# The last four routing tiles taken together, and three steps of exponentials in flight in self-attention

## The reference, cut to what matters

```python
# L0: route 1601 context rows into 2048 states, then a gated update
tok = ctx @ W_proj + b_proj
attn = softmax(x @ tok.T / 16)
routed = attn @ tok
ps_n, in_n = ln(x), ln(routed)
u, r = sigmoid([ps_n, in_n] @ W_u + b_u), sigmoid([ps_n, in_n] @ W_r + b_r)
cand = tanh([r * ps_n, in_n] @ W_n + b_n)
x = ln((1 - u) * x + u * cand)
# L1: a transformer block, 16 heads of 16
x = x + mha(ln1(x), ln1(x)); x = x + mha(ln2(x), ctx)
x = x + gelu(ln3(x) @ w1.T + b1) @ w2.T + b2
```

## Time and profile before

| what | value |
|---|---|
| median of 3 runs | 1500.87 us (1500.01 to 1504.94) |
| profiled execution, its own time | 1502.36 us |
| its span in the trace | 1500.7 us |
| mean granted TensorE clock | 0.967 |
| PE busy | 1397.3 us (93%) |
| ACT busy | 1095.9 us (73%) |
| DVE busy | 596.3 us (40%) |

### The profile page before, as it was taken

The page is one execution under the profiler, slowest core; times in us unless marked ns, Lnnn a source line. Parts: engine busy times, 40 slices in busy tenths (PEclk is TensorE's granted clock), DMA queues, the critical chain, the costliest instruction groups (busy, mean ns, idle before and its releaser), DMA issues.

```text
span 1500.7 us, 20741 instructions
## 1 busy us (share of the span) xinstructions
PE 1397.3 (93%) x8014; PEld 635.9 (42%) x8014; DVE 596.3 (40%) x1394; ACT 1095.9 (73%) x1350; POOL 48.7 (3%) x63
## 2 busy tenths in 40 slices
PE   7999989998669999999999999899898999899887
PEld 5667776776422223222322322222233433433346
DVE  5556576676740204312332340343342243144133
ACT  2533435444339999999999999789788797788843
POOL 2000000000010000000000000000000000000000
PEclk9999999998879999999999999899999999999999
DMA  9400001001249200100010353511000000000000
GB/s 305 164 34 1 1 0 57 1 1 57 89 117 126 67 16 19 26 28 11 12 53 12 45 118 47 119 36 35 13 23 15 23 12 12 23 15 1 5 11 15
DMA packets 35048, 66.06 MB, mean 44 GB/s; under 512 B 6202, under 2 KB 20092, under 8 KB 34204
## 3 DMA queue, kind: packets, MB, share of 16 engines
q1 hardware_dynamic: 29580, 43.24, 13.5%
q0 software_dynamic: 5360, 21.37, 3.9%
HBM read 42.70 MB, written 22.02 MB: 43 GB/s over the span
## 4 chain that ended last, share of the span: by engine, by line
PE 68%; ACT 22%; DVE 6%; issue 4%; DMA 1%; DVEq 0%; POOL 0%; SPq 0%; ACTq 0%; POOLq 0%
PE PS L1339 20%; ACT PX L897 20%; PE PS L1322 14%; PE PS L1421 3%; PE PS L1389 2%; PE PS L1139 2%; PE PS L1127 2%; PE PS L1370 2%; PE PS L1130 2%; PE PS L1056 2%; PE PS L1095 2%; PE PS L1096 1%; PE PS L1097 1%; PE PS L960 1%; PE PS L1404 1%
## 5 line engine op out<-in xcount | busy, mean ns | idle before, releaser
L897 ACT ACTIVATE PX<-PS 128x1024 f32<-128x1024 f32 (+1 forms) x928 | 881.7, 1040 | 119.6 <-PE PS L1322 73.3
L1339 PE MATMUL PS<-PX,V 128*32 128x512 f32 (+1 forms) x3712 | 499.3, 610 | 5.0 <-ACT PX L897 3.0
L1322 PE MATMUL PS<-QST,stack 50*128 50x512 f32 (+1 forms) x1856 | 385.5, 472 | 21.8 <-issue 13.5
L1322 PEld LDWEIGHTS PS<-QST,stack 50*128 50x128 f32 (+1 forms) x1856 | 156.8, 185 | 394.6 <-ACT PX L897 327.5
L1918 DVE COPY OT<-PS 128x512 f32<-128x512 f32 x32 | 22.1, 692 | 299.6 <-PE PS L1339 296.0
L1339 PEld LDWEIGHTS PS<-PX,V 128*32 128x32 f32 (+1 forms) x3712 | 73.7, 108 | 150.0 <-issue 111.6
L766 ACT ACTIVATE PH<-PS 128x512 fp32r<-128x512 f32 (+1 forms) x52 | 31.2, 600 | 82.7 <-PE PS L1076 73.2
L1421 PE MATMUL PS<-W,HIDT 128*128 128x256 f32 x192 | 47.8, 392 | 9.7 <-ACT HIDT L883 9.7
L1953 DVE RECIPROCAL REC<-REC 128x256 f32<-128x256 f32 x30 | 52.6, 1753 | 1.0
L782 ACT ACTIVATE TR<-PS,small 128x128 f32<-128x128 f32 x32 | 10.0, 363 | 56.7 <-PE PS L1130 56.7
L1421 PEld LDWEIGHTS PS<-W,HIDT 128*128 128x128 f32 x192 | 34.5, 189 | 33.7 <-issue 30.0
(11 more groups left out here) (209 smaller groups left out, 1574.2 us busy)
## 6 DMA issues: line engine op xcount, KB each, us to landing
QST<-q_parts SPq DMA_DIRECT2D x192, 64.0 KB
q_parts<-PARTS POOLq DMA_DIRECT2D x16, 512.0 KB, 3.5
stack<-k_parts SPq DMA_DIRECT2D x24, 200.1 KB, 6.8
stack<-k_parts SPq DMA_DIRECT2D x18, 256.0 KB
k_parts<-KPARTS POOLq DMA_DIRECT2D x8, 512.0 KB, 3.2
v_cross<-V POOLq DMA_DIRECT2D x1, 3328.0 KB, 11.8
V<-v_cross SPq DMA_DIRECT2D x2, 1664.0 KB, 13.6
k_parts<-PARTS POOLq DMA_DIRECT2D x6, 512.0 KB, 3.3
```

The source lines that it names most:

```text
L897: act.activation(PX[0:kr, (2 * t + half) % 4, :, :], PS[0:kr, slot:slot + 2, :], ACT.Exp, scale=SCALE).then_inc(at["exp"], 1)
L1322: ins = pe.matmul(PS[0:kr, 2 * (n % LOOK) + jj, :], KST[a][lo:lo + NROW, pair, kt * P:kt * P + kr].bitcast(F32R), QST[lo:lo + NROW, pair, ...
L1339: ins = pe.matmul(PS[32 * j:32 * j + 32, 6, :], V[0:kr, kt, 2 * (g // 2 * GH + j) + g % 2, :], PX[0:kr, (2 * t + j // 2) % 4, j % 2, :], s ...
```

## The change

1. **The last four tiles** (12 to 15) leave the slots: slots end at 15, and `last_tiles` on PE, ACT and DVE replaces slots 16 to 22. They are routed into four banks (6, 4, 5, 3) at once. DVE takes mean and variance from PSUM without dividing first, and one `rsqrt` over six values serves all four; ACT writes the normalised blocks (`routed_hat`) in place of DVE. Gates, candidates and finishes alternate between tiles, with CF4, XHS4, TR4, RPS4, TU4, CD4 and E4 (in the space of CHI, CLO and CN) as separate buffers. The projections of chunks 1 to 3 are placed anew.
2. **stage3** puts the k norm ahead of both q units, the banks rotate otherwise, and ACT's `split` no longer waits for `parts_ready`. For the first chunk `self_shift` drops a copy, and POOL stores its shift before the q parts of the last chunk. POOL's memset of V becomes eight smaller ones.
3. **Self-attention** gets six half-buffers (PX and PX2, which lies where KPARTS and W1 were), so ACT waits for pv(t-3). W1 is loaded after self-attention's last pv.
4. **PE's order in self-attention** becomes `scores(2t+2); pv(t-1); scores(2t+3); pieces`. The score slots rotate across chunk ends.
5. **REST[0]** spreads the pieces more widely.

```diff
-    {"y": [5, 8, 11, 14], "h": [21, 23], "u": [26, 28, 30, 32], "n": [38, 40]},
+    {"y": [6, 9, 12, 15], "h": [21, 24], "u": [27, 31, 38, 42], "n": [52, 56]},
...
-HAT_STEP = (16, 13)
+HAT_STEP = (17, 13)
...
+    PX2 = m.put("PX2", [P, 2, 2, CHUNK], F32, oW1)
...
+    def route_bank(i):
+        return 6 if i < FIRST_LAST else (6, 4, 5, 3)[i - FIRST_LAST]
+    def gate_bank(i):
+        return 7 if i < FIRST_LAST else (6, 4, 5, 7)[i - FIRST_LAST]
...
+    def score_slot(a, h):
+        return 2 * ((a * HALVES + h) % LOOK)
+    def exp_place(a, h):
+        if a == 1:
+            return PX[:, (h + 2) % 4]
+        return PX2[:, h % 6 - 4] if h % 6 >= 4 else PX[:, h % 6]
...
-                       enumerate(ks + vs[:2] + qs[:1] + norms[:1] + qs[1:] + vs[2:] + norms[1:])])
+        stage3.append([... enumerate(ks + vs[:2] + norms[:1] + qs + vs[2:] + norms[1:])])
...
-                sp.wait_ge(S["ln1_T"], TILES)
+            else:
+                sp.wait_ge(A[0]["pv"], HALVES // 2)
...
+                gp.wait_ge(S["l0_scaled"], 1)
+                for n in range(TILES // 2, TILES):
+                    gp.memset(v_parts(n, P)[:, :, 1:3, :], 1.0).then_inc(S["v_cleared"], 1)
...
+                if half and i == CHUNKS - 1:
+                    store_shift(0, 0, 0)
...
-            wait(act, S["parts_ready"], u - 1)
...
+        def routed_hat(i):
+            j = i - FIRST_LAST
+            act.wait_ge(S["l0_scaled"], 1)
+            act.activation(XHS4[:, j, 1, :], PS[:, route_bank(i), 0:D], ACT.Identity, scale=sm(SC4 + j),
+                           bias=sm(SB4 + j)).then_inc(S["l0_hat"], 1)
...
-                            wait(act, at["pv"], c * steps + t - 1)
+                            wait(act, at["pv"], c * steps + t + 1 - PLACES[a] // 2)
...
+        def last_tiles():                      # on PE
+            a, b, c, e = LASTS
+            for i in range(LAG):
+                l0_pv(STEPS - LAG + i)
+            gates(a - 1)
+            for i in LASTS:
+                route(i)
+            candidate(a - 1)
+            qkv(FIRST[0:2]); h_transposed(a - 3); qkv(FIRST[2:5])
+            hats(a); hats(b); gates(a); hats(c); gates(b); candidate(a); h_transposed(a - 2)
+            hats(e); gates(c); h_transposed(a - 1); candidate(b); gates(e); qkv(FIRST[5:6])
+            candidate(c); qkv(FIRST[6:8]); candidate(e); qkv(FIRST[8:]); qkv(SECOND[0:8])
+            for i in LASTS:
+                h_transposed(i)
+            qkv(SECOND[8:]); qkv(THIRD)
...
-                wait(pe, at["exp"], h - 1 if n < 2 else h - 2)
+                wait(pe, at["exp"], h - 2)
...
+                    if a == 0 and 2 * t + 3 < 2 * steps:
+                        scores(c, 2 * t + 3, first)
                     for o, kind, i, part, last in ev[t]:
...
-                    if 2 * t + 3 < 2 * steps:
+                    if a == 1 and 2 * t + 3 < 2 * steps:
                         scores(c, 2 * t + 3, first)
...
+        def last_tiles():                      # on DVE
+            norms(None, a - 2, a - 3); finish(a - 2, into=four[5]); gates(a - 1)
+            for i in LASTS:
+                routed_stats(i)
+            routed_scales(); next_hat(a - 2, AG4 + 10, NY4 + 5); candidate_sum(a - 1); new_state(a - 1, four[4])
+            rsqrt4(1, 4); finish(a - 1, AG4 + 8, NY4 + 4, four[6]); gates(a); qkv(FIRST[0:4]); gates(b)
+            candidate_sum(a); qkv(FIRST[4:5]); new_state(a, four[0]); rsqrt4(1, 6); next_hat(a - 1, ...); gates(c)
+            candidate_sum(b); new_state(b, four[1]); gates(e); candidate_sum(c); qkv(FIRST[5:6])
+            new_state(c, four[2]); candidate_sum(e); qkv(FIRST[6:8]); new_state(e, four[3]); rsqrt4(TPC)
+            finish(a, ...); qkv(FIRST[8:]); finish(b, ...); qkv(SECOND[0:2]); finish(c, ...); finish(e, ...)
+            rsqrt4(TPC); next_hat(a, ...); next_hat(b, ...); qkv(SECOND[2:5]); next_hat(c, ...); next_hat(e, ...)
+            qkv(SECOND[5:]); qkv(THIRD[0:2] + THIRD[4:5] + THIRD[2:4] + THIRD[5:])
```

More of the change, by code:

```diff
@@ L779, in reset @@
             act.wait_ge(S["l0_gates"], i + 1)
[L780 removed]
+            tr = work_of(i)[0]
+            if i < FIRST_LAST:
+                wait(act, S["l0_rps"], i)
             for c in range(2):
[L782 removed]
+                ins = act.activation(tr[:, c, :], PS[:, gate_bank(i), c * P:(c + 1) * P], ACT.Tanh, bias=sm(BRH + c),
+                                     scale=0.5)
             ins.then_inc(S["l0_rtanh"], 1)
@@ L809, in candidate @@
             act.wait_ge(S["l0_candz"], i + 1)
-            act.activation(CD[:], CZ[:], ACT.Tanh).then_inc(S["l0_cand"], 1)
+            _, _, _, _, cz, cd, _ = work_of(i)
+            act.activation(cd, cz, ACT.Tanh).then_inc(S["l0_cand"], 1)
+        def last_tiles():
+            a, b, c, e = LASTS
+            routed_out(CHUNKS - 1)
+            reset(a - 1)
+            update(a - 1)
+            for i in LASTS:
+                state_hat(i)
+            qkv(FIRST[0:2])
+            h_taken(a - 3)
+            for i in (e, a, b, c):
+                routed_hat(i)
+            candidate(a - 1)
+            concat(a)
+            concat(b)
+            reset(a)
+            update(a)
+            concat(c)
+            reset(b)
+            update(b)
+            candidate(a)
+            h_taken(a - 2)
+            concat(e)
+            reset(c)
+            update(c)
+            h_taken(a - 1)
+            candidate(b)
+            reset(e)
+            update(e)
+            qkv(FIRST[5:6])
+            candidate(c)
+            qkv(FIRST[6:7])
+            candidate(e)
+            qkv(SECOND)
+            for i in LASTS:
+                h_taken(i)
+            qkv(THIRD)
         def slot(k):
@@ L869, in slot @@
                 h_taken(h)
-        for k in range(SLOTS):
+        for k in range(TILES):
             slot(k)
@@ L1789, in candidate, with routed_stats, rsqrt4, routed_scales @@
-            stats(E2[:], 0, ch)
+            candidate_sum(g)
+            new_state(g)
+        def routed_stats(i):
+            j = i - FIRST_LAST
+            ve.wait_ge(S["l0_routed"], i + 1)
+            ch(ve.reciprocal(sm(RS4 + j), PS[:, route_bank(i), D:D + 1]))
+            stats(PS[:, route_bank(i), 0:D], j, ch, STAT4, AG4)
+        def rsqrt4(n, first=0):
+            rsqrt(n, ch, ag=AG4 + 2 * first, y=sm(NY4 + first, n), tmp=TMP4)
+        def routed_scales():
+            pairs = sm(AG4, 2 * TPC).rearrange("p (n two) -> p n two", two=2)
+            mean, var = (pairs[:, :, i:i + 1].rearrange("p n o -> p (n o)") for i in range(2))
+            for _ in range(2):
+                ch(ve.tensor_tensor(var, var, sm(RS4, TPC), ALU.mult))
+            rsqrt4(TPC + 2)
+            ch(ve.tensor_tensor(sm(SC4, TPC), sm(NY4, TPC), sm(RS4, TPC), ALU.mult))
+            ve.scalar_tensor_tensor(out=sm(SB4, TPC), in0=mean, scalar=-1.0, in1=sm(SC4, TPC), op0=ALU.mult,
+                                    op1=ALU.mult).then_inc(S["l0_scaled"], 1)
+            ve.wait_ge(S["l0_scaled"], 1)
@@ new lines, in last_tiles @@
+        def last_tiles():
+            a, b, c, e = LASTS
+            four = [(j, STAT4, AG4) for j in range(7)]
+            norms(None, a - 2, a - 3)
+            finish(a - 2, into=four[5])
+            gates(a - 1)
+            for i in LASTS:
+                routed_stats(i)
+            routed_scales()
+            next_hat(a - 2, AG4 + 10, NY4 + 5)
+            candidate_sum(a - 1)
+            new_state(a - 1, four[4])
+            rsqrt4(1, 4)
+            finish(a - 1, AG4 + 8, NY4 + 4, four[6])
+            gates(a)
+            qkv(FIRST[0:4])
+            gates(b)
+            candidate_sum(a)
+            qkv(FIRST[4:5])
+            new_state(a, four[0])
+            rsqrt4(1, 6)
+            next_hat(a - 1, AG4 + 12, NY4 + 6)
+            gates(c)
+            candidate_sum(b)
+            new_state(b, four[1])
+            gates(e)
+            candidate_sum(c)
+            qkv(FIRST[5:6])
+            new_state(c, four[2])
+            candidate_sum(e)
+            qkv(FIRST[6:8])
+            new_state(e, four[3])
+            rsqrt4(TPC)
+            finish(a, AG4, NY4, four[0])
+            qkv(FIRST[8:])
+            finish(b, AG4 + 2, NY4 + 1, four[1])
+            qkv(SECOND[0:2])
+            finish(c, AG4 + 4, NY4 + 2, four[2])
+            finish(e, AG4 + 6, NY4 + 3, four[3])
+            rsqrt4(TPC)
+            next_hat(a, AG4, NY4)
+            next_hat(b, AG4 + 2, NY4 + 1)
+            qkv(SECOND[2:5])
+            next_hat(c, AG4 + 4, NY4 + 2)
+            next_hat(e, AG4 + 6, NY4 + 3)
+            qkv(SECOND[5:])
+            qkv(THIRD[0:2] + THIRD[4:5] + THIRD[2:4] + THIRD[5:])
@@ L1795, in slot @@
             n = LT * b + (3 * j + 1 if j else 0)
-            if b >= CHUNKS:
-                norms(r, f, h)
-                gates(g)
-                finish(f)
-                qkv(LATE.get(k - 1, ()))
-                qkv(EARLY.get(k, ()))
-                candidate(g)
```

(1 more changed line is left out.)

233 lines of the change are left out of this document (137 added, 96 removed).

## The result

The changed kernel takes 1489.67 us (median of 5 runs, 1487.89 to 1492.73), the kernel before 1500.87. The ratio is 0.9931, with a 95% interval of 0.9913 to 0.9949. It is faster, by 11 us and not by the 27 of the forecast, and lies just above the forecast's range (1462 to 1488). The profiled execution took 1488.8 us, with a span of 1487.1.

What follows compares the result with a forecast made beforehand. Bounds: a chain hopping between engines in the tail, and self-attention near ACT's floor, losing time to PE's pieces. Gains 13.4 (tail) + 13.5 + 0.4 (self-attention) = 27.3 us off 1502.4; less 1.5 to the median, 1474 us, range 1462 to 1488.

Steps and rivals of the forecast that it cites:

- The tail: Last context product to first scores: 18.4 us shorter at full clock, less 5 for the clock, gains 13.4 us (6 to 18).
- (d): Tail: four times transpose and copy through bank 2, 5.4 us, ending at 401.3 us.
- (e): Tail: PE's last v, norms and THIRD take 13.6 us, with DVE behind it 15.6, ending at 416.9 us.
- the clock's share: Tail: 5 us (0 to 12) taken off for half clock, expected in part of (e) and something of an earlier stretch.
- (c): Tail: DVE's last new state, two rsqrt, four finishes and work between them, 19.6 us, ending at 395.9 us.
- R2: Rival: the tail stays as long and only self-attention gains, 1487 us; chance 0.08.
- R4: Slower rival: PE at 1.2 GHz from the tail's second stretch through (e), 10 us slower, 1511 us; chance 0.03.
- The gap from the flag to the first scores: End of the tail: 6.1 us for flag, register load and first matmul, claimed to stay.
- the ledger of self-attention: Tally of PE's lateness: pieces add cost, each step removes 0.18 us, ACT loses the excess; gain taken as 4.5 us a chunk.
- allowance of 1.25 us: Self-attention: PE lateness the three score slots tolerate after the change; new REST then loses 2.7 us a chunk.
- allowance of 0.27 us: Self-attention before: PE lateness tolerated with two buffer steps, fitted so the old REST loses 7.85 us against measured 7.5.
- R1: Rival: score slots, not PX, hold ACT; self-attention stays at 126 us, only the tail counts, 1487.5 us; chance 0.10.

Runs made afterwards that it cites:

- e10: Changed kernel with the first chunk's shift stored after the last q parts, as before: 1487.77 us, ratio 0.9892.
- e5: Changed kernel with the old order of scores and pieces, and the second u part at step 30 instead of 31: 1478.80 us, ratio 0.9841.
- e3: Changed kernel with the old order of scores and the old REST, keeping the third step of buffer: 1481.63 us, ratio 0.9862.
- e4: Changed kernel with only REST and HAT_STEP put back, keeping three steps of buffer and the new order: 1486.91 us, ratio 0.9915.
- e2: Changed kernel with only the old order of scores and pieces put back, keeping three steps and the new REST: 1481.35 us, ratio 0.9874.
- e7: Changed kernel with only the second u part moved, to step 30 instead of 31: 1485.27 us, ratio 0.9885.
- e6: e7 with both scores of a step issued side by side ahead of pv, pieces behind them: 1478.43 us, ratio 0.9841.
- e1: Changed kernel with self-attention's part put back (four places, old order, old REST), leaving the tail alone: 1490.63 us, ratio 0.9939.
- e11: Kernel before with e5's self-attention alone and W1's load moved, tail as before: 1490.06 us, ratio 0.9920.
- e9: e5 with three y pieces and both n pieces moved (y at 6, 10, 14, 16; n at 53, 55): 1479.52 us, ratio 0.9835.
- e8: Changed kernel with half of pv between the two scores of every step, so no two scores stand together: 1749.98 us, ratio 1.164.

## Why the prediction was wrong, step by step

**The tail was right in its sum, in part by luck.** The forecast had 13.4 us. From the last context product's start (326.06 before, 322.80 after) to the first scores (441.37, 424.72) it is 115.3 and 101.9 us, 13.4 less. Three timeline rows of the changed kernel, which answer to the earlier trace rows: the last copy of h, the last norm's reduction, the first scores.

```profile
401.22 0.81 ACT L804 ACTIVATE hF<-PS,cols 128x128 f32<-128x128 f32 x2 [0.90 <-PE PS L1133]
...
417.82 0.68 DVE L1834 TENSOR_REDUCE small<-PS 16x1 f32<-16x512 f32 x1
...
424.72 1.65 PE L1444 MATMUL PS<-QST,stack 50*128 50x512 f32 x6 [5.44 <-issue]
```

Windows from (d) of the prediction, the last four transposes, on: (d), then (e).

```profile
395.30:402.03 6.73, 3.58 (x11) 2.29 (x12) 4.37 (x9) 3.23 (x8) 1.45 (x2) 0.50 0.58 169
402.03:418.50 16.47, 13.59 (x40) 6.99 (x39) 9.96 (x19) 7.16 (x12) 3.43 (x5) 0.91 0.46 163
```

The tail itself began 3.26 us earlier than in the profile before, and the forecast counted from 326.3. On the forecast's scale the last copy ends at 402.0 + 3.3 = 405.3, where (d) had 401.3 before the clock's share. The last reduction ends at 418.5 + 3.3 = 421.8, where (e) had 416.9 and 5 for the clock, 421.9. So the 5 us that were set aside for the clock came out in sum, but not where they were put. The first of the four transposes starts at 395.30 + 3.3 = 398.6, where (c) ended at 395.9, so 2.7 us are there before (d), in a stretch with a granted clock of 0.91 to 0.97. That it is the clock's doing there is not shown. In (d) the clock is 0.50, and it takes 6.7 us in place of 5.4. In (e), where the forecast had most of the half clock, it is 0.91, and only 0.9 us are added. The granted clock of the tail was 0.88, up from 0.84. The last four transposes do stand together (L1133 at 395.30, 397.04, 398.75 and 400.46), each with its copy at 1.71 us, where the sum had 1.36. R2 (the tail stays as long) and R4 (half clock throughout) fall.

**The gap from the flag to the first scores stayed**, at 424.72 - 419.32 = 5.40 us from the decision's reduction (before, 441.37 - 436.10 = 5.27; the two reductions below, changed kernel and before), and the shift's load is not what ends it (e10).

```profile
419.32 0.16 DVE L2082 TENSOR_REDUCE small<-PS 1x1 f32<-1x16 f32 x1 [0.39 <-PE PS L1363]
...
436.10 0.16 DVE L1874 TENSOR_REDUCE small<-PS 1x1 f32<-1x16 f32 x1 [0.39 <-PE PS L1242]
```

**The step that failed is the ledger of self-attention**: with an allowance of 1.25 us the new `REST` was to lose 2.7 us a chunk, which, with a margin for pv, was taken as a gain of 4.5 us in each of three chunks. Measured is a gain of 0. Three terms of it were wrong:

- The allowance of 1.25 us. The prediction held that the wait for pv was the tight one and that the three score slots left room. It read one wait behind a y, 0.29 us for pv. But the kernel before has two there. Between the rows that the earlier trace rows show stands this one:

```profile
588.59 1.03 ACT L897 ACTIVATE PX<-PS 128x1024 f32<-128x1024 f32 x1 [0.34 <-PE PS L1322]
```

ACT waits 0.34 us for scores (L1322), and one exponential later 0.29 us for pv, and so behind all four y of the chunk. The allowance of 0.27 us was fitted to both losses together and put down to pv alone. The third step of buffer takes away only the second of them. What stays is the wait for scores, as e5 shows at the first y of a chunk:

```profile
556.85 3.80 ACT L992 ACTIVATE PX<-PS 128x1024 f32<-128x1024 f32 x4
560.99 2.86 ACT L992 ACTIVATE PX<-PS 128x1024 f32<-128x1024 f32 x3 [0.33 <-PE PS L1444]
```

The four exponentials start 0.91 us apart, and the next one comes 4.14 us after the first of them in place of 3.64. ACT so loses 0.50 us to a y of 1.06, and by the ledger's rule the allowance of the score slots is 0.56 us and not 1.25. The reason for the difference is that 1.25 was worked out for the first scores of two that stand side by side. The second can't be issued before one more exponential has ended, and behind it in PE's queue stand the pv of 1.00 us and the piece, before the scores that ACT needs next. The text saw that pv lowers the allowance and took only 0.6 us a chunk off for it. With 0.55 us the same ledger loses some 5.5 us a chunk with the old `REST` and 4.5 with the new (estimates, from the prediction's own costs). Measured, over the 118.6 us of its floor, are 5.1 (e3) and 4.1 (e5). The third step of buffer gains 2.4 us a chunk (e3), where the prediction's ledger gave 7.85 - 4.2 = 3.7 with the old `REST`.
- The order of the scores, which the sum priced at nothing. It is no free move: it parts pairs of scores that stood side by side, and a parted one costs 0.43 us of PE in place of 0.33. That is 0.2 us for every piece, and 1.8 to 2.2 us a chunk (e4 against e3, changed against e2, e7 against e5). The prediction named "if PE's step grows above 1.66 us with the new order of scores" among its failures. The plain step did not grow. The steps with a piece did, from 2.72 to 2.93 us. e6 shows that the cause is the parting, and not the place behind both scores.
- The copy of the head rows. The ledger counted PE's lateness alone. A u part at 31 puts 2.7 us of DVE's work ahead of a copy for which PE waits, and that costs 1.2 to 1.3 us a chunk (e5, e7), and 2.8 in the changed kernel's last, where half clock falls on it (1.3 in e10's). The prediction had looked at the other hand-over of the pieces, the bank that they share.

Together: 126.1 - 2.4 (buffer) + 2.1 (order), with the spread `REST` worth 1.05 us (e3's 123.72 to e5's 122.67) and the late copy 1.3 against it, gives 126.05, and 126.1 was measured. The first chunk, which has only sums, was to gain 0.4 us and gained 1.8 (120.1 to 118.3). Most of that comes with the third step of buffer too: e1 has 119.9 us there, e3 118.6. ACT's pass of 0.92 us, on which the floor was built, held: the changed kernel's first chunk of 118.3 us lies below the 121.1 that the rule of the Trainium skill would have made its floor ("ScalarE: Activation LUTs", section "What ACT_TABLE_LOAD costs", 0.946 us a pass).

The chance that went with self-attention staying at 126 us (R1, 0.10, 1487.5) had the right size and half of the cause. The slots do hold ACT once the third step is there (all waits of e3 are for scores), but at 123.7 us and not at 126.

**Cross-attention** was to be unchanged to 1 us. Its chunks are 111.4, 135.5, 130.1 and 129.2 us, where before they are 111.5, 131.7, 129.7 and 128.8, in all 4.5 us more. Their own code is the same but for W1's load and the numbering of the score slots and half-buffers, which e3 and e4 have too. Windows of 6 us behind the GELU of its second chunk, in the changed kernel:

```profile
1130.00:1136.00 6.00, 2.75 (x14) 1.77 (x10) 0.00 (x0) 5.97 (x4) 0.00 (x0) 0.89 0.00 0
1136.00:1142.00 6.00, 5.83 (x24) 1.22 (x22) 0.00 (x0) 4.27 (x5) 0.00 (x0) 0.50 0.24 68
1142.00:1148.00 6.00, 6.00 (x32) 3.29 (x32) 2.42 (x5) 2.68 (x3) 0.57 (x1) 0.75 0.00 0
```

In the kernel before:

```profile
1144.00:1150.00 6.00, 2.96 (x24) 0.56 (x20) 0.50 (x1) 5.86 (x3) 0.00 (x0) 1.00 0.00 0
1150.00:1156.00 6.00, 4.95 (x28) 2.47 (x32) 0.00 (x0) 5.97 (x8) 0.00 (x0) 1.00 0.17 50
```

In both PE stands for 3.25 us while ACT computes the GELU. In the kernel before the clock stays at 2.4 GHz behind it (1.00), in the changed one it falls to 1.2 GHz (0.50). The second chunk also took 134.2 to 135.8 us in e2 and in e5 to e11, all with the spread `REST`, and 131.7 to 132.6 in e1, e3 and e4, which have the old one. In the third and the fourth chunk the same holds: half clock behind the GELU in all nine kernels with the spread `REST`, in none of the four with the old one, and the third takes 130.0 to 130.2 us in place of 129.7. That is a correlation, in one trace of each kernel, and no cause is shown: the code behind these pauses doesn't depend on `REST[0]`, and e3 has its half clock elsewhere, in its first chunk (115.5 us, with a clock of 0.83 from 975 to 995 us). Nor is all of the second chunk's time lost at this pause. In the changed kernel 3.8 us are; in e5 2.9 of the 3.2 us are lost in the chunk's first steps, where the clock is at half from 1031.4 to 1042 us. What decides whether the clock falls in such a pause stays open. It moves a kernel by 3 to 4 us, which is why the chunks of the traces tell more here than the medians.

**The account** of the spans, 1500.7 to 1487.1: 3.3 us before the tail (the context products' end, which lies between 322.9 and 326.8 us in the kernels shown here, with the same work before it, so no gain of the change), 13.4 in the tail, 1.8 in the first chunk, -1.7 in the three others, -4.5 in cross-attention, and 1.3 behind the last exponential. That last stretch takes 50.4 to 50.8 us in six of the traces, the kernel before among them, and 49.2 to 49.3 in the other seven, also in e11, whose code there is that of before, so it is no gain of the change either.

**A version that is faster than both.** e5, the change with the order of scores as before and the u part at 30, takes 0.9841 of the kernel before; e6 and e9 can't be told from it. Against the changed kernel's 0.9931 that is some 0.9% more, and the intervals don't overlap. It is 24 us of 1503. The forecast's 27 were not reached by it either, since its chunks gain 3.4 us each and not 4.5.

## What to carry to other kernels

Before instructions are reordered, look at what stands side by side now, and read the price of each neighbourhood from starts: the same scores cost 0.33 us beside their like and 0.43 beside anything else. Where a buffer is made deeper, look for the other waits beside the one that it takes away: here the trace of before had a wait for scores ahead of each wait for pv, and it stayed. Work out the allowance for every instruction between the freed place and the next product, the second of two in a row too, and check it against such a wait. When pieces are spread over a loop, draw the queue of every engine that handles their results: a step that is free on PE may be just ahead of a copy on DVE for which PE waits.

## What the runs showed of the hardware

- Two pairs of scores (50x512) one after the other take 0.66 us from start to start. Apart, with a y, a u or a pv between, each takes 0.42 to 0.44 us (changed kernel, e8). Why is not shown.
- Four matmuls with 32 columns of weights, each into its own 32 rows of one bank (pv), take 1.00 us (changed kernel). Two of them by themselves take 0.99 us (e8).
- The clock may fall to half at a pause of PE of 3.25 us, or not: at the same pause behind the GELU it stayed at 1.00 in the kernel before and fell to 0.50 in the changed one.
- From the flag's decision to the first matmul behind it pass 4.9 to 5.4 us (5.27 before, 5.40 changed, 5.24 in e10, 4.90 in e11). The profile shows no work that PE waits for there.
